# Where GpSimd loads the next tokens: behind the normalising instead of ahead of the scalings

## The reference, cut to what matters

```
x = attn_layer(shift_tokens(x)) + x
x = ffn_layer(shift_tokens(x)) + x

attn_layer: q, k, v = x @ Wqkv            (16 heads of 64)
            q = l2norm(q) * q_scale ; k = l2norm(k) * k_scale
            q, k turned by rotary tables with a scale per position
            softmax over windows of 32 tokens and the window before, times v
            out @ Wo
ffn_layer:  layernorm, W1, a * gelu(gate), W2
```

## Time and profile before

| what | value |
|---|---|
| time, median of 3 runs | 3911.52 us (3907.31 to 3912.17) |
| the profiled execution | 3916.98 us |
| its span in the trace | 3915.2 us |
| PE busy | 3617.0 us (92%) |
| ACT busy | 3010.4 us (77%) |
| DVE busy | 2778.3 us (71%) |
| POOL busy | 2730.6 us (70%) |
| POOL L1519, `scale` | 768 times, mean 1043 ns |
| POOL L1475 and L1477, the load | 192 times each, means 393 and 397 ns |

### The profile page before, as it was taken

How to read it: one execution, slowest core, us unless ns; L and a number is a source line. 1 busy time by engine, 2 the same in 40 slices (tenths; PEclk the granted TensorE clock), 3 DMA queues, 4 the chain that set the end, 5 groups by cost and what they waited for, 6 DMA issues and landing times.

```text
span 3915.2 us, 94663 instructions
## 1 busy us (share of the span) xinstructions
PE 3617.0 (92%) x30894; PEld 2685.2 (69%) x30894; DVE 2778.3 (71%) x3770; ACT 3010.4 (77%) x6096; POOL 2730.6 (70%) x2889
## 2 busy tenths in 40 slices
PE   6898689999889999899999899999799999799998
PEld 3444367777667777677777677777577776577776
DVE  4566377776677776677776677776677776677776
ACT  3555478888688887688887688886688886788885
POOL 3454378886388884588884688883688882788872
PEclk7999789999999999899999899999899999899999
DMA  4223200000100000000001000001000001000002
GB/s 132 85 90 92 56 1 1 0 0 1 30 2 1 0 0 22 9 2 0 0 0 29 2 2 0 0 0 29 2 2 0 0 0 29 2 1 0 0 1 71
DMA packets 59745, 67.76 MB, mean 17 GB/s; under 512 B 12006, under 2 KB 40164, under 8 KB 58468
## 3 DMA queue, kind: packets, MB, share of 16 engines
q1 hardware_dynamic: 59492, 64.64, 5.8%
HBM read 46.27 MB, written 18.35 MB: 17 GB/s over the span
## 4 chain that ended last, share of the span: by engine, by line
POOL 41%; issue 29%; PE 19%; ACT 5%; DVE 3%; POOLq 2%; DMA 1%; SPq 1%; ACTq 0%; DVEq 0%
PE bank L401 16%; POOL sb_area L1505 16%; POOL sb_area L1519 12%; POOL sb_area L1527 6%; POOL sb_xs L1477 2%; POOL sb_xs L1475 2%; POOL sb_xwin L1484 2%; PE bank L614 2%; ACT sb_area L790 1%; DVE sb_area L1157 1%; ACT sb_area L940 1%; ACT sb_area L983 1%; DMA sb_wqk_lo<-qk_rows 1%; ACT sb_area L842 0%; ACT sb_lnb L952 0%
## 5 line engine op out<-in xcount | busy, mean ns | idle before, releaser
L790 ACT ACTIVATE sb_area<-bank 128x512 f32<-128x512 f32 (+4 forms) x2149 | 1315.2, 648 | 266.2 <-PE bank L614 206.4
L1236 DVE TENSOR_TENSOR sb_area<-bank,sb_rots 128x1024 f32<-128x1024 f32 x768 | 907.4, 1220 | 625.6 <-ACT sb_area L940 619.0
L1505 POOL TENSOR_TENSOR sb_area<-sb_area 128x512 f32<-128x512 f32 x768 | 983.6, 1281 | 311.8 <-DVE sb_area L1236 311.3
L401 PE MATMUL bank<-sb_area 128*64 128x64 f32 (+6 forms) x17104 | 1053.9, 276 | 10.2 <-DMA sb_area<-in_c_crot 3.5
L401 PEld LDWEIGHTS bank<-sb_area 128*64 128x64 f32 (+4 forms) x17104 | 750.0, 146 | 280.8 <-issue 244.0
L1519 POOL TENSOR_TENSOR sb_area<-sb_area,sb_rn 128x512 f32<-128x512 f32 x768 | 785.0, 1043 | 49.9 <-POOL sb_xs L1477 40.8
L401 PE MATMUL bank<-sb_area,sb_wvo 128*128 128x256 f32 x3072 | 728.3, 381 | 3.1 <-DVE sb_xT L1291 3.1
L401 PE MATMUL bank<-sb_wqk_hi,sb_xwin 128*128 128x512 f32 x1536 | 606.6, 436 | 43.0 <-POOL sb_xwin L1484 38.4
L614 PE MATMUL bank<-sb_ident,sb_area 128*128 128x128 f32 x3072 | 507.3, 288 | 134.1 <-POOL sb_area L1519 90.0
L401 PEld LDWEIGHTS bank<-sb_area,sb_wvo 128*128 128x128 f32 x3072 | 555.0, 190 | 75.2 <-issue 8.8
L614 PEld LDWEIGHTS bank<-sb_ident,sb_area 128*128 128x128 f32 x3072 | 330.9, 143 | 304.4 <-POOL sb_area L1519 211.7
(11 more groups left out here) (116 smaller groups left out, 4107.3 us busy)
## 6 DMA issues: line engine op xcount, KB each, us to landing
qk_rows<-sb_p SPq DMA_DIRECT2D x52, 256.0 KB, 4.2
sb_wqk_hi<-qk_rows SPq DMA_DIRECT2D x32, 256.0 KB, 2.9
sb_wqk_lo<-qk_rows SPq DMA_DIRECT2D x32, 256.0 KB, 2.7
sb_area<-in_Wqkv SPq DMA_DIRECT2D x7, 1024.0 KB, 5.7
sb_area<-in_WvT SPq DMA_DIRECT2D x7, 512.0 KB, 7.5
sb_wo_bd<-in_Wo SPq DMA_DIRECT2D x14, 256.0 KB, 8.5
sb_area<-in_x SPq DMA_DIRECT2D x4, 512.0 KB, 6.0
sb_area<-in_x SPq DMA_DIRECT2D x8, 256.0 KB, 2.9
```

What stands on the lines that cost most here:

```text
L401: return nc.tensor.matmul(o, a, b, start=start, stop=stop, skip_group_check=True)
L790: return nc.scalar.activation(o, i, ACT.Copy)
L1236: tt_(t12[:, c % 2, :, :].rearrange("p u (h d) -> p u h d", h=8), src, bc(rots[:, tt, s, :, :], [P, 2, 8, D], 2), ALU.mult).then_inc(S["ro ...
L1505: pt_(qn[:, c, :].rearrange("p (h e d) -> p h e d", h=8, e=2), t12[:, c % 2, 0, :].rearrange("p (h e d) -> p h e d", h=8, e=2), swapped, A ...
```

## The change

The call of `load_next` moves in the second half of a step from its place between `add(2)` and the scalings to the place between `normalise` and `add(3)`. Its first wait is another: in place of the third addition of the step it waits for the second scaling of the step, and for the normalising, where there is one. The two waits in `load_tile` stay as they are.

```diff
                     def load_next():
                         if v := behind(t, i, part, -2):
                             tt, bt = v
-                            pool.wait_ge(S["add"], (g_of(bt) * 4 + tt) * 4 - 4)
+                            pool.wait_ge(S["qn"], (g_of(bt) * 4 + tt) * 4)
+                            if last := behind(t, i, part, 2):
+                                pool.wait_ge(S["pn"], g_of(last[1]) * 8 + 2 * last[0] + 2)
                             load_tile(*v, not (part == 0 and t + 2 < TT))
...
                     for wp in range(2):
                         add(2 * wp)
-                        if wp == 1:
-                            load_next()
                         scale(1 - wp, 2 - 2 * wp)
                         scale(1 - wp, 3 - 2 * wp)
                         normalise(3 - wp, 1 - wp)
+                        if wp == 1:
+                            load_next()
                         add(2 * wp + 1)
```

## The result

The kernel after takes 3846.84 us (median of 4 runs, 3844.22 to 3850.08), the kernel before on the same chip 3911.85 (4 runs, 3907.31 to 3915.57). The ratio is 0.9835, with a 95% interval of 0.9818 to 0.9852: 65 us less. The forecast was 3857, with a range of 3830 to 3894.

The account below looks back on a forecast made before the run. ACT was taken to bound the first half, PE's work racing POOL's add(2), load, scaling the second. Terms 4.7 + 0.7 + 2.4 + 1.7 = 9.5 us a layer, 57 for six, gave 3860 or 3855; forecast 3857, range 3830 to 3894.

Parts of the forecast that it names:

- The way that bounds: Second half of a step: without the load between add(2) and the scalings, the scaling starts 1.57 us earlier.
- The full step: Loop steps followed by one of the same turn: second half 7.23 to 6.97, 18 x 0.26 = 4.7 us a layer.
- The jumps: Seven steps a layer ending at a loop jump: 0.1 us each, bounds 0 and 0.59, 0.7 a layer.
- The fill: Steps 0 to 4 of a layer: 2.4 us for steps 0 and 1, 1.7 for steps 2 to 4.
- the jump into the loop: Step 5, ending at the entry to the hardware loop: one of seven jumps at 0.1 us each.
- the term for step 2: Fill: gain limited by ACT's idle before its copy, 0.56 us, bounds 0 and 1.2.
- The cover: Behind the load's new place: add(3) keeps its distance from add(2), an extra wait and later tokens cost 0.
- The room of 0.54: Slack between add(3)'s end and DVE's rotation of chunk 1 in the next step: 0.54 us, 0.26 of it used.
- 1, PE is full: Full steps keep 14.38 us and only the fill gains: 3892 us, chance 0.13.
- 2, the first half shrinks too: Earlier normalising lets the first half fall to 6.95 us, 29 more gained: 3831 us, chance 0.10.
- 3, no effect: Something equally late takes over in the second half, such as ACT's copy or mask: 3917 us, chance 0.08.
- 4, slower: Load's wait for the normalising delays add(3) by 1.05 us and the rotation with it: 4009 us, chance 0.07.

Follow-up runs that it names:

- Experiment 3: Kernel before with one extra GpSimd operation (128x256, 0.61 us, result unread) added to the load in its old place: 3993.22 us, ratio 1.0212.
- experiment 2: Kernel after with the new place only in the written-out fill steps, the old place in the loop: 3890.18 us, ratio 0.9943.
- Experiment 11: Kernel after, unchanged, executed again for a second trace of the fill: 3845.27 us in one run.
- experiment 7: Kernel after without the load's waits for GpSimd's own scaling and normalising, order unchanged: 3849.12 us, ratio 0.9835.
- experiment 4: Kernel after with one extra GpSimd operation (0.61 us, result unread) added to the load in its new place: 3855.07 us, ratio 0.9859.
- experiment 8: Kernel after with ACT's rounding of token heads and GpSimd's rests_of_tile moved to the second half: 3830.08 us, ratio 0.9780.
- 9: Kernel after with GpSimd's rests_of_tile alone moved to the second half, behind add(2): 3853.41 us, ratio 0.9851.
- experiment 10: Kernel after with token heads and rests moved to the second half and the load put ahead of add(2): 3814.84 us, ratio 0.9752.

## Why the prediction was right, and where its sizes were off

**The way that bounds.** Right, and shown. The scaling comes 1.57 earlier behind `add(2)`, its weight load lies under `project_out`, and the second half is 6.96 for a forecast of 6.97. Experiment 3 shows the same way from the other side: 0.47 more on it are 0.47 more a step. The full step gained 0.28 for a forecast 0.26: 18 x 0.28 x 6 = 30 us for 28.

**The jumps.** Here the term was mis-sized: I took 0.1 for each, near the lower end of 0 to 0.59. Measured were 0.64 for the first jump of the loop, 0.44 for each of the five others (14.67 to 14.23), and 0.14 for the one into the loop in four of the six layers (14.37 to 14.23). The six inside are 0.64 + 5 x 0.44 = 2.8 a layer, 17 us, where the forecast had 3.6. This is 13 of the 16 us that the loop gave beyond its 32. By experiment 2, though, 4 of the 17 are not the load's: against jumps of 14.58 each is worth 0.35, 2.1 a layer and 13 us, still 9 more than forecast. So a jump hides the gain of the full step no more than any other boundary does: 0.28 of the 0.35 is the same 0.28. I had read the weight load's row, whose idle time was laid to "issue", and taken the missing name for a small price. PE's own row at the same place names POOL (0.19 at 2056.54), and I had not looked at it. Experiment 3 shows the same: a later scaling makes the jump period longer.

**The fill.** 17.9 and 19.4 us in two executions, for a forecast of 25 with the jump into the loop. By the starts of `add(2)`, averaged over the layers, steps 0 and 1 together went from 27.31 to 25.24, 2.1 for a forecast of 2.4; steps 2 to 4 from 43.05 to 42.11, 0.9 for 1.7. Step 4 went in most layers from 14.17 to 13.53, 0.64, near the forecast 0.56, but step 2 from 13.79 to 13.59 only. Experiment 11 shows that a fill differs by up to 4 us within one kernel, so the sum of six is not sure to some us. But step 2 is no accident: 13.79 stands in all layers with the old fill, and 13.59 is the median in three traces with the new one. So the term for step 2 was mis-sized, 0.56 for a measured 0.20, which is 2 us of the 6; it took ACT's idle before the copy as the next bound, and another wait came first. Which one stays open, and so does how much of the remaining 4 us is the clock's.

**The sum.** 57 were forecast and 65 measured; the loop's 16 more and the fill's 6 or 7 less make 66 by the trace. That the total came within 8 us is in part luck: the jumps were taken too low and the fill too high, and the two errors go against each other.

**The cover.** Right, and more ample than I had said. The load's own waits were hidden (experiment 7), as were the loaded tokens that come 3 us later. The room of 0.54 I had read at the rotation's start alone; 0.61 more put 0.21 of wait ahead of the rotation and nothing into the full step (experiment 4). The room ends sooner once ACT's head is out of the first half (experiment 8).

**The rivals.** 1, PE is full: wrong at 14.38, and also at 14.10, since experiment 10 comes to 13.92. The rule of the Trainium skill that would have it so is in TensorE: Matmul & The Clock Gate, The mechanism: weight loads overlap running products only if the row group differs. The trace contradicts it for this case: the weight load of 128 rows at 1974.91 starts together with the last product of 128 rows of `project_out`, and 0.22 before the next product (1975.13). 2, the first half shrinks too: it stayed at 7.14, as forecast, since ACT's chain holds it; experiments 8 and 9 show it, and behind a jump the wait of 0.31 at 1968.11 is laid to ACT. 3, no effect: refuted. 4, slower: the load's wait for the normalising exists, but it is 0.28 to 0.40 and not 1.05; in the loop of the kernel after no rotation waits for an addition, and the price shows only in experiment 8.

## What to carry to other kernels

When an engine's order is free, take off the way from a producer to its consumer whatever neither of them needs; for the steady step, where the piece goes matters little as long as a hole or slack is there (three places gave the same step; their fills differed). After such a move the next bound is often in the other half: look which engine works there without a hole, move its side job too, and put the moved piece into the idle time that opens. Where a row gives no releaser, read the row of the engine that does the work at the same instant before you price the hole near nothing. Where a row does name one, look up in the program which of its instructions is waited for: at `turn_qk(2)` the one named was not it. And when an order is changed in one part only, look at the periods of the part left alone: here they moved by 0.09 to 0.29.

## What the runs showed of the hardware

GpSimd's wait for its own last result left it idle for 0.22 to 0.41 in nearly all cases behind an operation of 128x512 (0.34 at 2010.95, 0.34 at 1976.07, 0.22 in experiment 3), and for 0.16 to 0.24 behind one of 64x128. Without such a wait the next instruction followed at once (experiment 7). An operation put in between did not hide the wait but had one of its own, 0.22; what it saved was 0.14 of its own 0.61 (experiment 3).

A weight load of 128 rows started with the last product of another weight, also of 128 rows, and the next product followed 0.22 later (1974.91, 1975.13), which is the spacing of the eight products before it (1.73 for eight). Where the weight load had to wait for GpSimd it followed 0.44 behind the last product.

In the fill, where PE has holes, the mean granted clock ranged from 0.86 to 0.94 in two executions of one kernel, and the time of one layer's fill by 4 us, while the loop's periods, at 1.00, repeated to 0.01 us.
